# A routed expert stage: how many blocks are routed ahead of the shared units, which engine makes h's second part, and how far ahead the next stage gathers

## What is computed

```python
logits = xt @ gate_w.T + gate_b
probs = jax.nn.sigmoid(logits)
w, idx = jax.lax.top_k(probs, TOP_K)            # 2 of 6 experts
w = w / (jnp.sum(w, axis=-1, keepdims=True) + 1e-08)
...
for e in range(N_EXPERTS):
    h = jax.nn.silu(xt @ ew1[e].T) * (xt @ ew3[e].T)
    y = y + ge[:, e:e + 1] * (h @ ew2[e].T)
z = jax.nn.silu(xt @ fc1.T) * (xt @ fc2.T) @ fc3.T      # the shared unit
...
x = x + 0.5 * _L0_ffn_ref(_layernorm(x, axis=-1), ...)
x = x + _L0_attn_ref(_layernorm(x, axis=-1), ...)
x = x + 0.5 * _L0_ffn_ref(_layernorm(x, axis=-1), ...)
x = x + 0.5 * _L1_ffn_ref(_layernorm(x, axis=-1), ...)
```

## Time and profile before

| | us |
|---|---|
| median of 3 runs (4530.1 to 4557.6) | 4552.2 |
| profiled execution, its own time | 4546.7 |
| its span in the profile | 4545.2 |
| PE busy | 3900.3 (86%) |
| DVE busy | 2931.7 (65%) |
| ACT busy | 2287.6 (50%) |
| POOL busy | 953.9 (21%) |

### The profile page before, as it was taken

The page is one execution under the profiler, slowest core; times in us unless marked ns, Lnnn a source line. Parts: engine busy times, 40 slices in busy tenths (PEclk is TensorE's granted clock), DMA queues, the critical chain, the costliest instruction groups (busy, mean ns, idle before and its releaser), DMA issues. The chain is left out here.

```text
span 4545.2 us, 74572 instructions
## 1 busy us (share of the span) xinstructions
PE 3900.3 (86%) x23584; PEld 2225.5 (49%) x23584; DVE 2931.7 (65%) x5431; ACT 2287.6 (50%) x4361; POOL 953.9 (21%) x1016
## 2 busy tenths in 40 slices
PE   6587769999999999995868696749999999996698
PEld 5476623333333333323657454626656566664454
DVE  6455778888888888825746453746656666662432
ACT  2144327777777777760235221316656566554222
POOL 4555600000000000001556430712212122220000
PEclk9799869999999999967889898959989899998799
DMA  4354643223233233104245311776767666652401
GB/s 76 56 163 144 214 60 47 39 40 47 32 47 43 36 47 42 22 3 106 24 113 170 115 38 36 213 171 184 188 168 187 173 177 192 180 151 64 136 4 37
DMA packets 217552, 452.77 MB, mean 100 GB/s; under 512 B 56922, under 2 KB 129626, under 8 KB 200410
## 3 DMA queue, kind: packets, MB, share of 16 engines
q1 hardware_dynamic: 179930, 358.80, 33.9%
q0 software_dynamic: 37248, 89.24, 7.5%
HBM read 272.59 MB, written 182.63 MB: 100 GB/s over the span
## 5 line engine op out<-in xcount | busy, mean ns | idle before, releaser
L1733 DVE TENSOR_REDUCE full_tops<-psum 128x1 f32<-128x1024 f32 x1024 | 1206.6, 1219 | 182.2 <-PE psum L1637 182.1
L1690 ACT ACTIVATE full_probs<-psum 128x512 f32<-128x512 f32 x2048 | 1066.4, 602 | 308.3 <-PE psum L1609 308.1
L2200 ACT ACTIVATE causal_probs<-psum 128x512 f32<-128x512 f32 (+3 forms) x1280 | 640.6, 533 | 405.1 <-PE psum L2072 233.0
L1609 PE MATMUL psum<-full_q,full_k 49*128 49x512 f32 x2048 | 659.0, 481 | 19.1 <-ACT full_probs L1690 13.1
L2251 DVE TENSOR_REDUCE causal_tops<-psum 128x1 f32<-128x1024 f32 (+7 forms) x704 | 586.9, 858 | 116.9 <-PE psum L2123 116.6
L1609 PEld LDWEIGHTS psum<-full_q,full_k 49*128 49x128 f32 x2048 | 288.3, 189 | 610.2 <-ACT full_probs L1690 568.5
L1618 PE MATMUL psum<-full_probs,full_vh 128*32 128x512 f32 x4096 | 565.4, 625 | 0.7 <-ACT full_probs L1690 0.7
L1637 PE MATMUL psum<-full_k,full_q 48*128 48x512 f32 x2048 | 404.2, 458 | 50.5 <-DMA full_k<-qk_split 22.8
L2072 PE MATMUL psum<-causal_q,causal_k 49*128 49x512 f32 (+3 forms) x1280 | 409.7, 453 | 14.4 <-ACT causal_probs L2200 8.3
L2123 PE MATMUL psum<-causal_k,causal_q 48*128 48x512 f32 (+4 forms) x1152 | 327.7, 416 | 69.0 <-DVE causal_tops L2266 32.4
L2025 POOL DMA_DIRECT2D band_scores<-xn x256 | 185.3, 724 | 851.8 <-DVE causal_tops L2266 851.8
(11 more groups left out here) (252 smaller groups left out, 6023.7 us busy)
## 6 DMA issues: line engine op xcount, KB each, us to landing
causal_bias<-bias_tiles SPq DMA_DIRECT2D x32, 1280.0 KB, 6.4
band_scores<-xn POOLq DMA_DIRECT2D x256, 160.0 KB, 4.8
moe_w_raw<-in_moe_w SPq DMA_DIRECT2D x44, 768.0 KB, 6.3
full_q<-qk_split SPq DMA_DIRECT2D x192, 128.0 KB, 6.1
full_k<-qk_split SPq DMA_DIRECT2D x192, 128.0 KB, 7.5
causal_q<-rot_parts SPq DMA_DIRECT2D x192, 128.0 KB, 5.3
causal_k<-rot_parts SPq DMA_DIRECT2D x192, 128.0 KB, 6.3
slot_outputs<-moe_y SPq DMA_DIRECT2D x42, 512.0 KB, 3.5
```

Of the source, the lines that this page charges most:

```text
L1609: nc.tensor.matmul(k.psum[:, b, :], k_sb[at, q, kt * P:(kt + 1) * P], q_sb[at, q, n * BLK:(n + 1) * BLK], start=True, stop=True).then_inc( ...
L1690: nc.scalar.activation(pT[:, kt % 4, n * BLK:(n + 1) * BLK], k.psum[:, bank(q, u), :], ACT.Exp).then_inc(p_ready, 1)
L1733: nc.vector.reduce_max(mx[:, q % 2, u // 2, u % 2:u % 2 + 1], src, AX_X).then_inc(m_free, 1)
L2200: nc.scalar.activation(dst, k.psum[:, bank(q, u), 0:(hi - lo) * P], ACT.Exp).then_inc(p_ready, 1)
```

## The change

1. **Four blocks ahead (`LOOK = 4`).** `xhi` and `xlo` have 5 buffers for 3. Blocks 0 to 3 are transposed, gated and chosen one after the other before `up(0)`, with positions(0) to positions(2) between them; in the loop behind it the shared unit of block v+1 stands beside the routing of block v+4. So positions(7) and `locate(7)` stand at the loop's fifth step, and three shared units behind them have no routing beside them. The positions of blocks 0 to 2 go to PSUM bank 4, so `transpose` waits for `pos_free` from block 4 on alone. The layer norm's steps move accordingly (`stats(3)` stands before `choose(0)`).
2. **h's low part on DVE (`lower_h`).** POOL's `rest` is gone in both parts of the stage. POOL's list is then only `pool_rstd`, scatters and gathers.
3. **Rows cast ahead of h.** On ACT the sigmoid and the cast of h are split; `upper_x` of the block ahead stands between them. On DVE `lower_h(v+1, 0)` stands behind `lower_x`.
4. **Buffer of the gathered rows.** `xg` is a view of the ring of the next stage, `ret_ring`, in place of a tile of its own.
5. **Next stages.** The first `pool_rstd` stands behind the gathers of 6 tiles (12 DMAs) for 8, the second behind 6 more (full attention) or 2 more (LSTM); in the LSTM the DVE adds 4 tiles and takes their statistics, twice, for 8 tiles at once.

```diff
-        xhi = sb("x_hi", [P, 3, C, BLK], F32R)
-        xlo = sb("x_lo", [P, 3, C, BLK], F32R)
+        xhi = sb("x_hi", [P, 5, C, BLK], F32R)
+        xlo = sb("x_lo", [P, 5, C, BLK], F32R)
...
-        xg = sb("xg", [P, 4, TB, D])
+        xg = ret.ring[:, :, :, :].rearrange("p (r a) b d -> p r (a b) d", r=4)
...
+        LOOK = 4
+
+        def pos_bank(n):
+            return 4 if n < LOOK - 1 else 7
...
-                rest(0, 0)
-                rest(0, 1)
-                for v in range(NBLK - 2):
-                    rest(v + 1, 0)
-                    rest(v + 1, 1)
-                    if v + 4 < NBLK:
-                        ln.pool_rstd(pool, v + 4, v % 2)
-                    scatter(v + 1)
...
+                for n in range(NBLK):
+                    scatter(n)
+                    if n + 4 < NBLK:
+                        ln.pool_rstd(pool, n + 4, n % 2)
+                for b in range(NX):
                     gather(b)
...
-                positions(0)
-                transpose(1)
-                gate(1)
-                gate_transpose(1)
+                for n in range(1, LOOK):
+                    transpose(n)
+                    positions(n - 1)
+                    gate(n)
+                    gate_transpose(n)
                 up(0, 0)
                 up(0, 1)
-                for v in range(NBLK - 2):
+                for v in range(NBLK - LOOK):
                     up(v + 1, 0, (0,))
-                    positions(v + 1)
+                    positions(v + LOOK - 1)
                     up(v + 1, 0, (1,))
-                    transpose(v + 2)
+                    transpose(v + LOOK)
                     up(v + 1, 1)
-                    gate(v + 2)
+                    gate(v + LOOK)
                     down(v, 0)
-                    gate_transpose(v + 2)
+                    gate_transpose(v + LOOK)
                     down(v, 1)
...
                 for v in range(NBLK, NV):
                     if v + 1 < NV:
-                        hidden(v + 1, 0)
+                        sigmoid(v + 1, 0)
                     if v + 2 < NV:
                         upper_x(v + 2)
                     if v + 1 < NV:
-                        hidden(v + 1, 1)
+                        upper_h(v + 1, 0)
+                        sigmoid(v + 1, 1)
+                        upper_h(v + 1, 1)
...
+                def lower_h(v, m):
+                    u = 2 * v + m
+                    dve.wait_ge(hh_ready, u + 1)
+                    nc.vector.tensor_tensor(h_lo[:, v % 2, m, :], hf[:, u % 2, :], h[:, v % 2, m, :].bitcast(F32),
+                                            ALU.subtract).then_inc(hl_ready, 1)
...
-                ret.pool_bring(pool, 0, 2 * TB)
+                ret.pool_bring(pool, 0, TB + 2)
                 ln.pool_rstd(pool, 0, 0)
-                ret.pool_bring(pool, 2 * TB, TB)
+                ret.pool_bring(pool, TB + 2, TB + 2)
                 ln.pool_rstd(pool, 1, 1)
```

More of the change, by code:

```diff
@@ L826, in _ @@
                 stats(2)
+                stats(3)
                 choose(0)
@@ L829, in _ @@
                 weigh(0)
-                locate(0)
                 rest(0)
-                lower_x(1)
-                apply(2)
-                stats(3)
-                choose(1)
-                weigh(1)
+                for n in range(1, LOOK):
+                    lower_x(n)
+                    locate(n - 1)
+                    apply(n + 1)
+                    if n + 3 < NBLK:
+                        stats(n + 3)
+                    choose(n)
+                    weigh(n)
                 hidden(0, 0)
+                lower_h(0, 0)
                 hidden(0, 1)
-                for v in range(NBLK - 2):
-                    locate(v + 1)
+                lower_h(0, 1)
+                for v in range(NBLK - LOOK):
+                    locate(v + LOOK - 1)
                     hidden(v + 1, 0)
-                    lower_x(v + 2)
-                    if v + 3 < NBLK:
-                        apply(v + 3)
+                    lower_x(v + LOOK)
+                    lower_h(v + 1, 0)
+                    if v + LOOK + 1 < NBLK:
+                        apply(v + LOOK + 1)
                     hidden(v + 1, 1)
-                    choose(v + 2)
-                    weigh(v + 2)
+                    lower_h(v + 1, 1)
+                    choose(v + LOOK)
+                    weigh(v + LOOK)
                     update(v)
-                    if v + 4 < NBLK:
-                        stats(v + 4)
+                    if v + LOOK + 3 < NBLK:
+                        stats(v + LOOK + 3)
                 locate(NBLK - 1)
                 schedule()
-                hidden(NBLK - 1, 0)
-                hidden(NBLK - 1, 1)
-                update(NBLK - 2)
+                for v in range(NBLK - LOOK, NBLK - 1):
+                    for m in range(C):
+                        hidden(v + 1, m)
+                        lower_h(v + 1, m)
+                    update(v)
                 rest(1)
@@ L861, in _ @@
                 rest(3)
-                hidden(NBLK, 0)
-                hidden(NBLK, 1)
+                for m in range(C):
+                    hidden(NBLK, m)
+                    lower_h(NBLK, m)
                 address()
@@ L2704, in _ @@
         def _(pool):
-            def both(m):
-                for t in range(2):
-                    ln.pool_rstd(pool, m + t, t)
             for n in range(NBK):
                 if ret and n == 0:
-                    ret.pool_bring(pool, 0, 2 * TB)
-                both(n * 2)
+                    ret.pool_bring(pool, 0, TB + 2)
+                ln.pool_rstd(pool, n * 2, 0)
+                if ret and n == 0:
+                    ret.pool_bring(pool, TB + 2, TB - 2)
+                ln.pool_rstd(pool, n * 2 + 1, 1)
                 if ret and n + 1 < NBK:
@@ L2820, in normalize @@
             def normalize(n):
[L2821 to L2823 removed]
                 for t in range(2):
+                    if ret:
+                        ret.dve_add(dve, (2 * n + t) * TB, TB)
+                        dve.wait_ge(k.added, ret.run * TT + (2 * n + t + 1) * TB)
                     ln.dve_stats(dve, n * 2 + t, t, n * TB + t * (TT // NB))
```

91 lines of the change are left out of this document (42 added, 49 removed).

## The result

The changed kernel takes **4405.9 us** (median of 4, 4396.2 to 4419.8) where the kernel before takes 4548.6 us (median of 4, 4530.1 to 4557.6) beside it. The ratio is 0.9695 with a 95% interval of 0.9659 to 0.9731, so the gain is between 122 and 155 us. The forecast was 4428 us, a gain of 124; the result is 22 us under it and 1 us above the lower end of the stated range, 4405 to 4478. Six executions on another chip gave 4403.2 us against 4548.6 and a ratio of 0.9688 (0.9652 to 0.9724).

What follows compares the result with a forecast made beforehand. PE was taken to bound the experts' part, and a chain of routing, scatters, landing, lists and gathers the routing's end. Gains 38.9 + 34.9 + 50 = 124 us took the median from 4552.2 to 4428 us, range 4405 to 4478.

Steps and rivals of the forecast that it cites:

- The transitions: Routing up to PE's first gathered rows: the last block's scatters start earlier, gaining 38.9 us in run 0, 34.9 in run 1.
- The two reliefs on DVE: Routing step of 19.75 us: 2.9 us off for `choose`'s stall, 1.2 off for the wait for the cast of x.
- the 15.3 for a step without statistics: Routing loop: three of four steps take 15.3 us each, shorter than 16.3, but PE's own work comes close.
- 22.9 us from the last block's first scatter to the lists: End of routing, run 0: this length stays as before, since everything behind the last block's first scatter keeps its length.
- the scatters' landing bounds the routing: Rival, 12%: landing limits the routing part; at 17 us a step 18.5 us per run are lost, 4465 us.
- the rival of late shared units: Rival, 5%: PE's shared units, starting 18 us later at half clock, end after the rows come; 4458 us.
- PE bounds it, with some 31 us lost: Experts' part: PE is busy 202.9 of 234 us and waits regularly, mostly for the low part of x.
- The 0.8 us "to spare": Experts' block: low part of x ready at 296.6, 0.8 us before PE's `down` ended at 297.4, so the wait goes.
- The size 25: Experts' part: 25 us gained in each run, of 27.1 us of PE's waits in run 0; 50 us together.
- the lock: Experts' block: DVE's weights' low part, which stood still while POOL's `rest` ran, falls from 2.98 to 1.76 us.
- The lock rule's price: Last block's scatters: `lower_h` could hold up POOL's DMA issues, costing up to 2 x 1.2 us of the sum.
- Parts 4 and 5: Gathered rows' buffer 0; next stages' shorter leads between 0 and 5 us per stage, taken as 0.

Runs made afterwards that it cites:

- run 1: Not an experiment: the second of the feed-forward's two runs within one execution; its experts' part took 233.0 us before, 202.8 in the changed kernel.
- the experiments with late weights: Changed kernel, first two experts' weight loads moved behind the lists: both 4401.0 us (4487.6 on another chip), the second alone 4482.2 us there.
- the late cast: Changed kernel with the cast of x behind that of h on ACT, as before: 4480.4 us, ratio 0.9841 to the kernel before.
- run 0: Not an experiment: the first of the feed-forward's two runs within one execution; its experts' part took 233.8 us before, 202.7 in the changed kernel.
- the long leads: Changed kernel with 8 tiles gathered ahead of the next stages' first rstd instead of 6, as before: 4406.3 us in one execution.

## Why the prediction was right, and where it was not

**The transitions: size right, two terms off against each other.** `up(0)` starts at 57.5 (59.7 expected), `locate(3)` at 68.4 (71.0). The four steps take 56.9 us and not 62.2: 15.7 with the statistics and 13.5, 14.0, 13.7 without. The two reliefs on DVE seem well sized, as 15.7 for an expected 16.3 suggests, though the clock differed in this step too. The term that failed is the 15.3 for a step without statistics, which was held up by "PE's own work comes close". That was read at a granted clock of 0.87, with PE busy 78.9 us in five steps of before, 15.8 in each; here the clock is 1.00 and PE is busy 52.7 us in four, 13.2 in each. It does not hang on the order of four ahead: with two ahead the steps without statistics took 13.5 to 14.0 us too. `locate(7)` is at 125.4 (133.2 expected) and the last scatters at 126.9 (134.5).

What was won there was lost in "22.9 us from the last block's first scatter to the lists", which is 33.4 us (run 1: 28.2). The prediction kept this length because it saw no change behind the scatters. But the two loads of weights changed their place. Before, POOL's `rest` held up the scatters, so the loads (168.34 on SP) went out 5 us ahead of the first of them. Now they go out 4.3 us behind it. The rival "the scatters' landing bounds the routing" named the right place with the wrong cause, and the experiments with late weights settle it. From the lists to PE's rows are 14.1 us (13.9 expected).

PE's shared units end at 153, not 164. With rows at 174.5 PE stands 21.4 us, where under 12 was expected. The half clock feared for the front did come, but briefly. The first products of `up(0)` take 0.63 us, as those of the gates ahead of it do, and from 61.5 us on they take 0.39 (the changed kernel's record of the clock begins only at 71.9):

```profile
58.06 0.63 PE L496 MATMUL psum<-moe_x_lo,moe_w_hi 128*128 128x512 f32 x1
...
61.70 0.39 PE L496 MATMUL psum<-moe_x_lo,moe_w_hi 128*128 128x512 f32 x1
```

So the rival of late shared units had its condition but not its effect.

**The experts: right direction, wrong bound.** The step that failed is the first sentence on them, that "PE bounds it, with some 31 us lost". A ring of DVE and ACT bounded it at 11.13 us per block, and PE's waits were the difference to its own 9.24. The prediction cut 2.4 us from the path to the low part of x and added `lower_h` behind it for nothing, since it "lies behind `lower_x`". In the ring the bill is 1.23 us for the low part of the weights, 1.25 for the cast and 0.60 back for one `lower_h`: 1.88, and with 0.01 from the last link the 1.89 between 11.13 and 9.24. The 0.8 us "to spare" were none in the ring, as the late cast showed. Ring and PE are even by coincidence. By the bill, half a microsecond more on DVE would have made the gain less (an estimate, not run), and no margin in front of PE would have told so.

The size 25 was too small, since it took PE's 202.9 us busy as the floor. That sum was itself stretched: the same 1176 matmuls are busy 197.3 us now, at a granted clock of 0.98 for 0.97. Idle time fell by 25.7 us (31.15 to 5.43) and busy time by 5.6.

The share of the parts was seen wrong too. The prediction gave the cast's move 1.2 us of 2.4 and the lock the other half. Without the cast's move (x cast late) the experts' part gains 8.2 and 7.1 us; without `lower_h` on DVE 20.9 and 25.9. The cast is the greater part, because it takes two casts out of the ring and also moves POOL's subtraction away from the low part of the weights.

**The lock rule's price did not come.** From the Trainium skill's page "SBUF — State Buffer", section "Who interferes with whom", the prediction took that `lower_h` could hold up POOL's DMA issues. The same section infers that a `tensor_tensor` on DVE leaves free the interface that descriptor generation needs. For `lower_h` no run shows a hold-up: the last block's 8 scatters take 9.8 us (126.89 to 136.7) with `lower_h` beside them, as in run 1 of the kernel before (11.0 in run 0, with the one issue of 2.15 us). For the weights' low part the traces do show one, against that inference. In the experts' part of run 0 ten of the 84 issues take 1.3 to 2.5 us for 0.95, nine of them beside DVE's low part of the weights (267.14, 1.87 us, is one). PE has no wait for rows behind the second block, so none of them costs time.

**Parts 4 and 5** were taken at 0 between 0 and 5. No run takes part 4 out alone. For part 5 the long leads show nothing beyond noise. Behind run 0 the reason given holds: the first wait is shorter and the one behind it longer by as much.

**Signs named ahead.** `choose` has no instruction over 0.4 us (0.31 where 3.22 stood), the weights' low part is 1.76 us for all 19, the waits before `up` are gone, the experts' part is 203 us (209 expected). The lists at 160 (157 expected) stayed within 165. Missed: PE's wait under 12 us, and the last block's first scatter near 134 (126.9), since the steps were shorter.

## What to carry to other kernels

Before a wait is read as the loss of the engine that waits, follow the engines that feed it through one whole period and add up the starts. If the sum of links that never touch the waiting engine is the period, they are the bound, and its slack means nothing: here a move of 1.25 us was worth 1.26 us per block although 1.2 us of slack stood in front of PE.

Where a wait is taken out, list what else was issued around it on other queues, for bulk loads above all. They keep their own time, and a few loads that used to go ahead of small transfers can come to stand in the midst of them.

## What the runs showed of the hardware that was not expected

The stall between POOL's and DVE's instructions goes by phase. With both kinds of work still running in each block, DVE's low part of the weights took 2991 ns in the median in one order of ACT's list and 1763 ns in the mean in the other. There POOL's DMA issue beside it took up to 2.5 us for 0.95: the stall changed sides.

PE's granted clock in the routing loop was 0.87 before, that is, partly the lower level of 1.2 GHz, and 1.00, 2.4 GHz throughout, in the changed kernel. PE's busy share alone does not tell which: between 100 and 150 us PE was busy 41.8 us at 0.83 in the kernel before and 42.1 us at 0.97 in the one with two blocks ahead. That kernel had 1.00 between 60 and 100 us, so the order of four ahead is not needed for it. What decides it stays open.

On one chip the last block's scatters started 22 to 25 us later than on the others with the same lists of instructions up to there, while the kernel before was only 24 us slower there in all. Its cause was not found.
